# A reordered front, and transposing transfers in place of TensorE's transposes, in a fused attention and mixture-of-experts kernel

## The reference

```python
q1 = fake_quant(layernorm(x), x1_scale, x1_zp)      # round, clip to 0..255
q2 = fake_quant(ctx, x2_scale, x2_zp)               # ctx: 2 x 1024 x 1024
x = x + tanh(g_xattn) * (q1 @ q2)                   # per batch: 512x1024 @ 1024x1024
xt = layernorm(x)                                   # 1024 tokens
scores = softmax(xt @ router_w + router_b) + router_bias        # 16 experts, 4 groups
# best 2 of 4 groups, in them the best 2 experts
y = sum over the 2 experts of score * ((silu(xt@w1+b1) * (xt@w2+b2)) @ w3 + b3)   # inner 256
z = (silu(xt@sw1+sb1) * (xt@sw2+sb2)) @ sw3 + sb3   # shared expert, inner 512
x = x + tanh(g_ffn) * (y + z)
```

## Time and profile before

| | |
|---|---|
| median of three runs | 430.03 us |
| profiled execution, device time | 433.93 us |
| its span, first to last instruction | 432.2 us |
| TensorE, VectorE, ScalarE, GpSimd busy | 366.7, 216.5, 164.2, 74.8 us |
| chain of work that ended last | PE 62%, DVE 14%, DMA 12%, issue 5%, ACT 3% |
| mean granted TensorE clock | 0.954 of full speed |
| moved by DMA | 58.31 MB, mean 135 GB/s |

### The profile page before, as it was taken

One profiled execution on the slowest core, in us unless ns is written; L12 is line 12 of the kernel. 1 busy time (PEld: TensorE's weight loads), 2 busy tenths in 40 slices (PEclk: granted clock), 3 DMA queues, 4 the chain that ended last, 5 costly groups with the idle time before them and its releaser, 6 DMA issues.

```text
span 432.2 us, 7630 instructions
## 1 busy us (share of the span) xinstructions
PE 366.7 (85%) x2438; PEld 186.9 (43%) x2439; DVE 216.5 (50%) x429; ACT 164.2 (38%) x228; POOL 74.8 (17%) x75
## 2 busy tenths in 40 slices
PE   0199388789899999999799889999789979999950
PEld 0154288644444464444344344444335434444410
DVE  2868844987988437775555942111154531111100
ACT  1466443846624223111134533333266433333311
POOL 3100400250013300000200102222122222222211
PEclk9999689999899999999999969999998969999995
DMA  8993412338303320000794144446896461545543
GB/s 311 374 313 91 153 50 86 113 97 288 102 2 130 161 99 2 2 0 0 257 327 181 64 148 99 99 97 154 242 283 194 130 152 20 111 109 103 118 86 49
DMA packets 30539, 58.31 MB, mean 135 GB/s; under 512 B 3014, under 2 KB 19470, under 8 KB 30512
## 3 DMA queue, kind: packets, MB, share of 16 engines
q1 hardware_dynamic: 25604, 40.14, 27.4%
q0 software_dynamic: 4896, 17.83, 17.6%
q10 hardware_dynamic: 12, 0.00, 0.0%
HBM read 41.19 MB, written 16.78 MB: 134 GB/s over the span
## 4 chain that ended last, share of the span: by engine, by line
PE 62%; DVE 14%; DMA 12%; issue 5%; ACT 3%; POOL 1%; ACTq 1%; POOLq 0%; DVEq 0%
PE PS L1364 16%; PE PS L1561 11%; PE PS L1375 10%; DMA area<-split_dram,tok 7%; PE PS L1536 7%; PE PS L1314 6%; DMA out_dram<-rows,row 4%; PE PS L1502 3%; DVE stats L773 2%; DVE areaW L827 2%; ACT rows L703 2%; PE PS L1538 2%; PE PS L1377 1%; DMA sc<-in_g_ffn_dram 1%; DVE areaW L1187 1%
## 5 line engine op out<-in xcount | busy, mean ns | idle before, releaser
L1364 PE MATMUL PS<-areaT,areaW 128*128 128x128 f16 (+1 forms) x672 | 87.4, 294 | 6.7 <-DVE areaT L858 3.5
L1561 PE MATMUL PS<-areaW,area 128*128 128x512 f16 x384 | 88.7, 389 | 0.0
L1364 PEld LDWEIGHTS PS<-areaT,areaW 128*128 128x128 f16 x672 | 51.8, 101 | 40.4 <-DVE areaT L858 3.9
L1561 PEld LDWEIGHTS PS<-areaW,area 128*128 128x128 f16 x384 | 37.9, 101 | 43.8 <-issue 4.1
L1536 PE MATMUL PS<-areaT,areaH 128*128 128x512 f16 x192 | 48.4, 389 | 2.7 <-DVE areaH L1212 1.7
L490 POOL DMA_INDIRECT out_dram<-rows,row x16 | 25.9, 1620 | 132.0 <-ACT rows L703 105.7
L1375 PE MATMUL PS<-SW,areaH 128*128 128x512 f16 x192 | 44.2, 380 | 2.3 <-DVE areaH L867 2.3
L1257 DVE TENSOR_TENSOR areaH<-PS,areaH 128x256 f32<-128x256 f32 x16 | 6.8, 424 | 62.6 <-ACT areaH L725 62.6
L472 POOL DMA_INDIRECT area<-split_dram,tok x18 | 18.0, 1000 | 104.5 <-ACT tok L678 98.7
L1314 PE MATMUL PS<-area,areaQ 128*128 128x512 f16 x128 | 32.6, 411 | 2.2 <-DVE r L831 1.2
L1192 DVE COPY area<-PS 128x1024 f16<-128x1024 f16 x17 | 11.7, 689 | 37.8 <-PE PS L1502 36.1
(11 more groups left out here) (228 smaller groups left out, 436.3 us busy)
## 6 DMA issues: line engine op xcount, KB each, us to landing
ring<-in_L_ffn_sw_dram SPq DMA_DIRECT2D x12, 512.0 KB, 4.9
X<-in_x_dram SPq DMA_DIRECT2D x8, 512.0 KB, 6.0
areaT<-in_ctx_dram SPq DMA_DIRECT2D x8, 512.0 KB, 10.1
ring<-in_ctx_dram SPq DMA_DIRECT2D x8, 512.0 KB, 4.3
out_dram<-X SPq DMA_DIRECT2D x8, 512.0 KB, 3.1
areaT<-in_L_ffn_ew_dram SPq DMA_DIRECT2D x4, 1024.0 KB
wrow<-in_L_ffn_ew_dram SPq DMA_DIRECT2D x4, 1024.0 KB, 5.8
ring<-in_L_ffn_ew_dram SPq DMA_DIRECT2D x4, 1024.0 KB, 8.0
```

The lines of the kernel that those rows point to most:

```text
L1364: last = mm(PS[:, 4 + 2 * (c % 2) + w, lo:hi], SW[:, wp, 2 * c + w, k, :], XT[:, xp, k, tk], start=(k == 0 and n == 0), stop=(k == KC - 1 ...
L1561: mm(PS[:, 4 + j, :], XGT[j][:, xp, k, :], W12S[j][:, wp, k, :], start=(k == 0 and n == 0), stop=False)
```

## The change

Three things are changed.

**The front's order.** `bn(0)` runs before the scalars are waited for, and the coefficients of tiles 0 and 1 are made one by one. ScalarE runs an idle Silu first. `evac_q1` of tiles 0 and 1 goes to ScalarE. TensorE takes the first products per tile. The low halves of chunks 2 and 3 leave GpSimd for VectorE, and the four first low halves are spread between `attend`, `bn` and `ln2_lo`. `add_r1` goes from GpSimd to ScalarE, after the last `ln_rows`. GpSimd keeps only the powers, gathers and scatters.

**The blocks of batch 0.** `first_blocks(i)` multiplies the high weights of all four chunks with tile i, then turns tile i+1, then multiplies the low weights. Both copies of a turned tile are on ScalarE.

**Transposing transfers.** For the q tiles 4 to 7, the norm rows of tiles 4 to 7 and all gathered tiles, TensorE's transposes and both copies from PSUM are replaced by `dma_start_transpose`. SP issues those of q and of the norm rows, ScalarE those of the gathered tiles. In the loop the gather is issued three tiles ahead; it waits for the turn that frees its buffer. The turn of tile a+2 is issued in step a, behind the gate.

```diff
+            def turn_q1(i):                                    # SP
+                sp.wait_ge(x_q, i + 1)
+                if i == TB:
+                    sp.wait_ge(at_done, TB)
+                sp.dma_start_transpose(Q1T[:, i % TB, :, :], QB[:, i % 2, :]).then_inc(q1t_in[i % 2], 16)
+            def turn_tokens(i):
+                sp.wait_ge(ln_hi, i + 1)
+                sp.wait_ge(ln_lo, i + 1)
+                sp.dma_start_transpose(XT[:, :, :, i * P:(i + 1) * P].rearrange("p h k t -> p (h k) t"), WROW[i])\
+                    .then_inc(xt_in[i - TB], 16)
...
+            for r in range(9, 12):
+                load_chunk(r)
+            turn_q1(TB)
+            turn_q1(TB + 1)
+            load_chunk(12)
+            turn_q1(TB + 2)
+            turn_q1(TB + 3)
+            for r in range(13, len(CHUNKS)):
                 load_chunk(r)
             for i in range(TB, NT):
+                turn_tokens(i)
                 store_split(i)
...
             def gather(t, j):                                  # GpSimd
                 pool.wait_ge(tok_rdy, t + 1)
                 pool.sem_inc(gathers, 1)
+                if not (isinstance(t, int) and t < 2):
+                    pool.wait_ge(xgt_in[j], 8 * t - (0 if j == 0 else 8))
+                    pool.sem_inc(gathers, 1)
...
             def step(a, j):
-                gather(a + 2, j)
+                gather(a + 3, 1 - j)
...
+            def add_r1(b):                                     # ScalarE
+                act.wait_ge(r1_rdy, b + 1)
+                for i in range(b * TB, b * TB + TB):
+                    nc.scalar.activation(X[:, i, :], X[:, i, :], ACT.Identity, bias=r1[:, i:i + 1]).then_inc(x_r1, 1)
+            def turn_tokens(t, j, count):
+                act.wait_ge(tok_in[j], count)
+                act.sem_inc(waited, 1)
+                if not (isinstance(t, int) and t < 2):
+                    act.wait_ge(up_done, t - 1)
+                    act.sem_inc(waited, 1)
+                act.dma_start_transpose(XGT[j].rearrange("p h k t -> p (h k) t"),
+                                        XG[j].rearrange("p h n -> p (h n)")).then_inc(xgt_in[j], 16)
...
-                act.wait_ge(xg_T, 2 * a + 2)
-                tokens_of(a + 2, j)
-                tokens_low(a + 1, 1 - j)
+                act.wait_ge(tok_in[1 - j], 8 * a + (16 if j == 0 else 24))
+                act.sem_inc(waited, 1)
+                tokens_of(a + 3, 1 - j)
...
                 nc.scalar.activation(HSP[j][:, 0, :], HF[j], ACT.Copy, scale=HS / UPS).then_inc(h_hi, 1)
+                turn_tokens(a + 2, j, 8 * a + (32 if j == 0 else 24))
...
+            dve.wait_ge(x_in[0], 16)                           # VectorE
+            bn(0)
             dve.wait_ge(small_in, 96)
...
+            link(v.reciprocal(cf[:, 3:4], sc6[:, 0:1]))
+            coefs(0, 1, cf[:, 3:4], None, sc6[:, 1:2])
...
+            dve.wait_ge(x_in[1], 16)
+            bn(1)
+            clamp_x(0)
+            coefs(1, 1, cf[:, 3:4], None, sc6[:, 1:2])
...
-            for c in range(2):
-                lo_chunk("sw", c)
+            clamp_ctx(0, 7)
             attend(0)
             bn(0)
             attend(1)
             coefs(0, 1, None, XS, None)
             bn(1)
+            lo_chunk("sw", 0)
             ln2_lo(0)
-            tk_hi_evac(0)
             coefs(1, 1, None, XS, None)
             attend(2)
+            lo_chunk("sw", 1)
...
+            def first_blocks(i):                               # TensorE
+                tk = slice(i * P, (i + 1) * P)
+                for c in range(2):
...
+                    for w in range(2):
...
+                        for k in range(KC):
+                            for xp in range(2):
+                                mm(PS[:, 4 + 2 * c + w, tk], SW[:, 0, 2 * c + w, k, :], XT[:, xp, k, tk],
+                                   start=(k == 0 and xp == 0), stop=False)
+                if i < TB - 1:
+                    transpose_tokens(i + 1)
+                for c in range(2):
+                    for w in range(2):
+                        pe.wait_ge(*lo_done(2 * c + w))
+                        for k in range(KC):
+                            last = mm(PS[:, 4 + 2 * c + w, tk], SW[:, 1, 2 * c + w, k, :], XT[:, 0, k, tk], start=False,
+                                      stop=(k == KC - 1))
...
             for i in range(TB, NT):
-                transpose_tokens(i)
-                if i == TB:
-                    pe.wait_ge(at_read, NT)
-                router(i - TB)
...
+                pe.wait_ge(xt_in[i - TB], 16)
+                router(i)
...
-                transpose_gathered(a + 1, 1 - j, 8 * a + (16 if j == 0 else 24))
...
-                pe.wait_ge(xg_hi, a + 1)
-                pe.wait_ge(xg_lo, a + 1)
+                pe.wait_ge(xgt_in[j], 8 * a + (16 if j == 0 else 8))
```

More of the change, by code:

```diff
@@ L481, in _ @@
             gather(1, 1)
+            gather(2, 0)
             def scatter(t, j):
@@ L533, in _ @@
                 act.dma_start(sc1[n:n + 1, 0:1], scalars[n].rearrange("(a n) -> a n", a=1)).then_inc(small_in, 16)
+            act.wait_ge(consts, 5)
+            nc.scalar.activation(cf[:, 13:14], mhalf[:, 0:1], ACT.Silu)
             act.wait_ge(sc_rdy, 1)
@@ L608, in _ @@
             quant_x(0)
+            quant_ctx(0, 0)
             quant_x(1)
-            quant_ctx(0, 0)
+            evac_q1(0)
+            quant_ctx(0, 1)
+            evac_q1(1)
             quant_x(2)
-            quant_ctx(0, 1)
+            quant_ctx(0, 2)
             quant_x(3)
-            for k in range(2, KC):
+            for k in range(3, KC):
                 quant_ctx(0, k)
@@ L651, in _ @@
                 ln_rows(i)
-            for i in range(TB, NT):
-                tk_lo_evac(i)
+            add_r1(0)
+            add_r1(1)
             act.wait_ge(lg_sub, 1)
@@ L1163, in _ @@
                 sd_evac(i)
-            for i in range(TB, NT):
-                tk_hi_evac(i)
             route()
@@ L1325, in row_sums @@
             def row_sums(b):
-                pe.wait_ge(q1_rdy, TB * (b + 1))
+                if b == 0:
+                    pe.wait_ge(q1_rdy, TB)
+                else:
+                    for j in range(2):
+                        pe.wait_ge(q1t_in[j], 32)
+                    pe.wait_ge(at_read, TB)
                 for j in range(TB):
@@ L1494, in _ @@
                 shared_down(TB + i)
-            def transpose_gathered(t, par, count):
-                pe.wait_ge(tok_in[par], count)
-                for h in range(2):
-                    if not (isinstance(t, int) and t == 0):
-                        pe.wait_ge(xg_hi if h == 0 else xg_lo, t)
-                    for k in range(KC):
-                        last = nc.tensor.transpose(bank16(2 + h)[:, k, :], XG[par][:, h, k * P:(k + 1) * P], idh[:, :])
-                    last.then_inc(xg_T, 1)
-            pe.wait_ge(sd_read, NT - 2)
-            transpose_gathered(0, 0, 16)
             pe.wait_ge(empty_rdy, 1)
```

286 lines of the change are left out of this document (127 added, 159 removed).

## The result

| | kernel before | changed kernel |
|---|---|---|
| median (runs) | 431.56 us (4) | 410.65 us (4) |
| lowest, highest | 428.68, 434.49 | 406.97, 415.7 |
| profiled execution, its span | 433.93, 432.2 us | 406.97, 405.0 us |
| mean granted TensorE clock | 0.954 | 0.95 |

The ratio is 0.952, 95% interval 0.947 to 0.958: 20.9 us faster by the medians, where 43.7 were forecast. The predicted 387 us was missed, and the median lies above its range, which ended at 405. The two profiled spans differ by 27.2 us.

A forecast was written before the change was run, and what follows sets the result against it. It took the chain of waits to lie mostly on TensorE, then VectorE. Terms summed to 43.7 us off the profiled 433.93, 390.2; 386.3 for the median, given as 387, range 373 to 405.

The forecast's parts named there:

- To the first attention result: Front: earlier statistics and quantisation, evacuations on ScalarE and low halves moved bring the result from 39.31 to 32.3, 7.0 us.
- Norm rows and the blocks of the first half: Front: without GpSimd's low halves 2.9 us; reordered products, q turns off TensorE and shorter waits 8.3 us together.
- Turned q and norm rows: Transposing transfers before the loop: q turns off TensorE 1.8 us, 0 to 2 lost waiting; norm rows' turns beside routers 5.1.
- landings over 11 us: Sign of being wrong: turning transfers landing this late, where 3 to 7 us were expected.
- Loop entry: Start of the expert loop: VectorE's chain decides the first down product; 4.2 us gained, between 2.7 and 7.
- The loop, 16.2: Expert loop: 13 tiles lose 0.9 us each, 11.7, and stalls shrink; 16.2 us gained, between 0 and 24.
- covers an issue from 0.4 to 5 us: Loop: ScalarE, busy 13.99 of 41 us in four tiles, idles 6.7 in each, enough for issuing a turn.
- an issue over 5 us: Sign of being wrong: ScalarE's issue of one turning transfer taking longer than this.
- The stalls: Loop: 13.7 us above the steady beat from tile 2 to tile 14, of which 9.2 were expected to remain.
- the earlier gather removes most stalls: Rival for the loop: gathering three tiles ahead brings loop 24 and entry 7, 376 us; chance 0.08.
- the scatter becomes the beat: Rival for the loop: scatters beside turns land in 7.5 to 9.5 us, the loop gains nothing, 403 us; chance 0.12.
- More than forecast: Rival in which the earlier gather removes most stalls: loop 24, entry 7, 376 us; chance 0.08.

The follow-up runs named there:

- f1_front: The changed front with every turn back on TensorE and the loop of the kernel before: 414.76 us, 0.960 of the kernel before.
- l3_hold: l0_free plus one extra ScalarE instruction per loop step, holding its queue 3.6 us without DMA load: 411.80 us.
- l9_late_hold: l6_copy_hold with copy and hold moved behind the row evacuation and selection column in ScalarE's step: 405.55 us.
- l0_free: f1_front with the changed kernel's loop, a 4 KB transfer replacing each gathered tile's turn (wrong values, all waits kept): 398.53 us.
- l12_two_part: l1_act_copy plus a second copy of a quarter the size on ScalarE's queue, right behind the first: 415.25 us.
- l7_copy_hold_relax: l6_copy_hold with the row evacuation waiting only for the scatter two tiles back: 408.41 us.
- l6_copy_hold: l1_act_copy plus the extra ScalarE instruction of l3_hold, so load and an even 3.6 us hold together: 412.19 us.
- l1_act_copy: l0_free with a plain copy of the gathered tile in 252-byte pieces, issued by ScalarE, in the turn's place: 402.66 us.
- l10_double_load: l1_act_copy plus a second plain copy of the same size per tile, issued by ScalarE right behind the first: 420.20 us.
- l8_long_hold: l6_copy_hold plus one more ScalarE instruction per step, adding 1.04 us of hold: 422.89 us.

## Why the prediction was wrong, point by point

- **To the first attention result, 7.0:** 6.0 measured (39.31 to 33.33). Right.
- **Norm rows and the blocks of the first half, 2.9 and 8.3:** second products 19.0 us earlier against 18.2 by the sum. Right. The low row takes 1.22 to 1.23 us in all eight tiles now, where one took 2.92. The rule on the shared port pair in the Trainium skill, SBUF — State Buffer, section "SBUF: two separate sides", agrees with this.
- **Turned q and norm rows:** TensorE waits for neither; the routers of tiles 0 to 7 take 3.2 us (134.51 to 137.73), for 3.3 in the sum. f1_front and its kin, which turn these on TensorE, reach the first row evacuation at 238.3 to 241.5, the changed kernel at 231.92: 6.4 to 9.5 us for the 6.9 (1.8 + 5.1) of the sum. SP's q turns landed in 3.2 to 4.9 us, the norm rows' in 4.3 to 5.0. In the loop the last packet of a turn came 3.8 to 11.4 us after its issue began, so the prediction's sign of being wrong, landings over 11 us, was met once. The estimate of 21 us for sixteen blocks one after another, from the Trainium skill, VectorE: DVE Perf Modes, section "The three transpose paths", is not what these rows show. 512 KB in 2.84 us of all engines is 185 GB/s. The Trainium skill, DMA: Bandwidth & Descriptors, section "Latency and other measured facts", gives 261 GB/s, which this trace doesn't reach.
- **Loop entry, 4.2:** together with the front 26.9 of 27.5. Right.
- **The loop, 16.2: wrong, 0.3 with the tail.** The step that failed is the sentence that ScalarE's idle 6.7 us per tile "covers an issue from 0.4 to 5 us". It holds for tiles without weights and issues below 5 us: beside issues of 2.80 to 4.85, TensorE keeps its 9.27 us from 335.75 to 372.82. It fails in three ways. The 6.7 was read in the window 362 to 403, four tiles without weights; where weights are split, ScalarE has 5.9 us more work, and l3_hold loses 13.3 us with an even hold of 3.62. The issue isn't constant: three of the sixteen in the loop took 6.3 to 7.3 us, so the prediction's sign of an issue over 5 us was met. And an idle share says nothing of the place in the queue, which l9_late_hold shows to count for about half.
- **Where the loss lies:** of the 15.0 us between the changed kernel's stretch and that of l0_free, 5.5 are in three steps with the weights' halves (288.40 to 326.80, 38.4 us for 32.9), 3.1 in two steps before (241.93 to 263.60), and 5.0 in three after (335.80 to 366.78), which TensorE meets only at the end, as a wait of 4.59 us for a row evacuation at 386.85. The two longest issues, 7.32 and 6.83 us, cost next to nothing: their steps take 12.37 and 12.43 us, and 12.26 and 12.36 in l0_free, because the row evacuation waits for the scatter before it in both. And some 5 us of the 15.0 are TensorE's clock: it is busy for 142.1 us from 232 to 394 in the changed kernel, and for 136.9 from 239 to 386 in l0_free, with 613 and 615 matmuls. The prediction had no term for this.
- **The growing hold** was no term of the prediction. I had costed the issue as a constant and the load by whether the engines' time fits. l12_two_part, with both, has the stretch of the changed kernel within 2.1 us. How the 15 us between the changed kernel and l0_free divide between the two in the turn itself is not settled, as no experiment varies one of them in a turn.
- **The stalls:** I left 9.2 of 13.7 us, and gave 11.7 to the turns that left TensorE. l0_free reached my total by another split: 7 to 10 us from the earlier gather, 6 to 9 from the turns, whose full 10.5 come only once the wait for the scatter is relaxed. The rival that the earlier gather removes most stalls was right on its mechanism and got 0.08.
- **The rivals:** "the scatter becomes the beat" named the loop's gain of nothing (403 us) but not its cause; l7_copy_hold_relax gives its wait 4 to 5 us of l6's 13.7. Theory 3's wait (8.6 us on GpSimd) wasn't tried by itself. In the trace of after, little hangs on it: the turn at 382.10, which waits for a gather held up in this way, begins 2.0 us behind the gate, and the row evacuation after it waits for a scatter until 385.20 in any case.
- **The range:** its lower end, 373, is not what its terms give. With loop and entry at their upper bounds the time is 376, as the rival "More than forecast" has it. The outcome lies at the other end.

## What to carry to other kernels

- Read an engine's slack in the tiles where it is busiest, and at the place of the new instruction in its queue, not as an idle share of a quiet window.
- A transfer can cost its issuer, too. A plain copy of 504 KB alone held it for 0.6 us, a second one right behind it for 1.1 to 10.3, and a turning transfer for 1.6 to 7.3. Put such an issue behind what others wait for, and look at what stands behind it on any engine that is to issue it, SP included.
- Before a resource is relieved, try to start earlier what it waits for: one more gather in flight was worth about as much as all turns taken off TensorE, and added 0.5 MB to 58.3.

## What the runs showed of the hardware that I had not expected

- The issue of a plain transfer of 504 KB in 252-byte pieces took 0.614 to 0.659 us on ScalarE with nothing close before it (l1_act_copy); the next one on the same queue, right behind it, took 1.1 to 10.3 us for the same size (l10_double_load) and 1.1 to 8.4 us for a quarter of it (l12_two_part). So the size of the one that waits made no difference that these runs show.
- A turning transfer of 512 KB held ScalarE for 1.6 to 7.3 us by itself, and SP, in the four of the norm rows, for 1.5 to 3.1. Four of 256 KB on SP took 1.23 to 2.40.
- ScalarE's 3.6 us of hold in sixteen steps cost 13.3 us (l3_hold over l0_free), and 1.04 us more cost 10.7 (l8_long_hold over l6_copy_hold).
